# Router split moved from VectorE to ScalarE and GpSimd, and new work orders for the front of a cross-attention and expert kernel

## What is computed

```python
def _L0_xattn_ref(texto, imagen, Wq, bq, Wk, bk, Wv, bv):
    q = texto @ Wq + bq
    k = imagen @ Wk + bk
    v = imagen @ Wv + bv
    scores = jnp.einsum('bqd,bkd->bqk', q, k) * scale
    attn = jax.nn.softmax(scores, axis=-1)
    return jnp.einsum('bqk,bkd->bqd', attn, v)

def _L0_ffn_ref(x, w_router, w_gating, w_gate, w_up, w_down):
    router_probs = jax.nn.softmax(jnp.einsum('bsh,he->bse', x, w_router), axis=-1)
    gate_weights = jax.nn.softmax(jnp.einsum('bsh,he->bse', x, w_gating) / GATE_TEMP, axis=-1)
    g = jnp.einsum('bsh,ehf->ebsf', x, w_gate)
    u = jnp.einsum('bsh,ehf->ebsf', x, w_up)
    h = jax.nn.silu(g) * u
    expert_out = jnp.einsum('ebsf,efh->ebsh', h, w_down)
    cw = router_probs * gate_weights
    cw = cw / (jnp.sum(cw, axis=-1, keepdims=True) + 1e-09)
    return jnp.einsum('ebsh,bse->bsh', expert_out, cw)
x = x + _L0_xattn_ref(_layernorm(x, axis=-1), ctx_1024, ...)
x = x + _L0_ffn_ref(_layernorm(x, axis=-1), ...)
```

## Time and profile before

| | us |
|---|---|
| median of 3 runs | 983.49 (982.96 to 984.57) |
| profiled execution, its time | 983.63 |
| its span, first to last instruction | 981.8 |
| TensorE busy | 972.3 |
| VectorE busy | 751.7 |
| GpSimd busy | 671.1 |
| ScalarE busy | 483.8 |

### The profile page before, as it was taken

The page is one execution under the profiler, slowest core; times in us unless marked ns, Lnnn a source line. Parts: engine busy times, 40 slices in busy tenths (PEclk is TensorE's granted clock), DMA queues, the critical chain, the costliest instruction groups (busy, mean ns, idle before and its releaser), DMA issues.

```text
span 981.8 us, 16527 instructions
## 1 busy us (share of the span) xinstructions
PE 972.3 (99%) x6167; PEld 925.7 (94%) x6167; DVE 751.7 (77%) x1355; ACT 483.8 (49%) x857; POOL 671.1 (68%) x514
## 2 busy tenths in 40 slices
PE   8999999999999999999999999999999999999998
PEld 7899999999999999999999999999999999999998
DVE  6987456877788777787777877778877788777785
ACT  6788564453544444444535444444445454444441
POOL 3789976866767576676667675766767676767642
PEclk9999999999999999999999999999999999999999
DMA  8341140010101001010101010010100010100002
GB/s 213 85 140 46 36 150 22 22 43 3 43 22 43 23 22 43 22 44 23 36 9 44 22 44 22 22 43 22 44 22 24 21 44 23 43 22 23 1 1 76
DMA packets 37352, 40.63 MB, mean 41 GB/s; under 512 B 2644, under 2 KB 35272, under 8 KB 37272
## 3 DMA queue, kind: packets, MB, share of 16 engines
q1 hardware_dynamic: 37264, 39.58, 13.6%
q10 hardware_dynamic: 8, 0.00, 0.0%
HBM read 35.90 MB, written 3.67 MB: 40 GB/s over the span
## 4 chain that ended last, share of the span: by engine, by line
PE 97%; DMA 1%; DVE 1%; SPq 1%; issue 0%; ACT 0%; DVEq 0%
PE ps L280 94%; DMA w_raw<-in_L_ffn_w_up 1%; PE ps L1556 1%; PE ps L1584 1%; DVE wr_split L284 0%; DVE arena L284 0%; PE ps L1627 0%; PE ps L1601 0%; SPq L294 0%; PE ps L1545 0%; SPq L328 0%; PE ps L1652 0%; SPq L339 0%; SPq L324 0%; DVE xsacc L1264 0%
## 5 line engine op out<-in xcount | busy, mean ns | idle before, releaser
L280 PE MATMUL ps<-arena 128*128 128x256 f32 (+3 forms) x3120 | 415.2, 285 | 2.6 <-DVE arena L284 2.2
L280 PEld LDWEIGHTS ps<-arena 128*128 128x128 f32 (+2 forms) x3120 | 404.2, 190 | 9.7 <-DVE arena L1085 1.7
L488 POOL TENSOR_TENSOR arena<-shared,arena 128x448 fp32r<-128x448 f32 x196 | 250.8, 1295 | 192.6 <-ACT arena L825 185.7
L280 PE MATMUL ps<-xc_hi,w_hi 128*128 128x448 f32 x904 | 331.7, 367 | 0.0
L280 PE MATMUL ps<-xc_hi,w_lo 128*128 128x448 f32 x904 | 330.2, 365 | 0.0
L280 PE MATMUL ps<-xc_lo,w_hi 128*128 128x448 f32 x904 | 329.7, 365 | 0.0
L818 ACT ACTIVATE shared<-shared 128x448 f32<-128x448 f32 x180 | 101.4, 579 | 191.8 <-DVE shared L1204 124.9
L280 PEld LDWEIGHTS ps<-xc_hi,w_lo 128*128 128x128 f32 x904 | 169.8, 188 | 13.8
L280 PEld LDWEIGHTS ps<-xc_hi,w_hi 128*128 128x128 f32 x904 | 170.5, 189 | 10.5
L280 PEld LDWEIGHTS ps<-xc_lo,w_hi 128*128 128x128 f32 x904 | 170.6, 189 | 10.2
L1198 DVE TENSOR_TENSOR shared<-ps,shared 128x448 f32<-128x448 f32 x60 | 37.5, 624 | 110.9 <-PE ps L280 110.9
(11 more groups left out here) (152 smaller groups left out, 1103.4 us busy)
## 6 DMA issues: line engine op xcount, KB each, us to landing
early<-in_L_ffn_w_down SPq DMA_DIRECT2D x16, 512.0 KB, 4.0
shared<-in_ctx SPq DMA_DIRECT2D x16, 336.0 KB
w_raw<-in_L_ffn_w_gate SPq DMA_DIRECT2D x17, 256.0 KB, 2.9
w_raw<-in_L_ffn_w_up SPq DMA_DIRECT2D x17, 256.0 KB, 3.3
early<-in_L_ffn_w_gate SPq DMA_DIRECT2D x15, 256.0 KB, 2.8
early<-in_L_ffn_w_up SPq DMA_DIRECT2D x15, 256.0 KB, 3.2
x_dram<-xsacc SPq DMA_DIRECT2D x8, 224.0 KB, 2.7
xsacc<-x_dram SPq DMA_DIRECT2D x1, 1792.0 KB, 7.5
```

The lines of the kernel that those rows point to most:

```text
L280: ins = nc.tensor.matmul(dst, w, m, start=first and i == 0, stop=last and i == len(passes) - 1, skip_group_check=onto)
L488: nc.gpsimd.tensor_tensor(h[:, 1, j, at:at + TC], tile, h[:, 0, j, at:at + TC].bitcast(fp32), ALU.subtract).then_inc(hid_lo_done, 1)
```

## The change

Three things are done. The router's split leaves VectorE: its copy becomes ScalarE's `router_high`, its subtraction GpSimd's `router_low`. Its transfer, `load_router`, moves in the SP queue from behind the first context to behind the last part of x. And the hand-laid lists of calls of SP, GpSimd, ScalarE, VectorE and TensorE are written in another order, up to the first experts' tiles. The number of `keep_busy` calls stays ten; eight stood before `transpose_weights(1)`, now four do, and six stand between `queries(0)` and `transpose_ctx(3, 0)` (two before).

```diff
-            load_x(0)
             load_weights(0)
             load_weights(1)
+            load_x(0)
+            load_ctx_half(0, 0)
             load_x(1)
-            load_ctx_half(0, 0)
+            load_bv()
             load_ctx_half(0, 1)
+            load_ctx_half(1, 0)
+            load_set(0)
+            load_x(2)
+            load_ctx_half(1, 1)
+            load_wv()
+            load_x(3)
+            load_ctx(2, 0)
             load_router()
...
+            def router_low():
+                pool.wait_ge(wr_hi_done, 1)
+                nc.gpsimd.tensor_tensor(wr_split[:, :, 1, :], wr_raw[:], wr_split[:, :, 0, :].bitcast(fp32),
+                                        ALU.subtract).then_inc(wr_done, 1)
...
+            def router_high():
+                sc.wait_ge(router_in, 2 * DMA)
+                nc.scalar.copy(wr_split[:, :, 0, :], wr_raw[:]).then_inc(wr_hi_done, 1)
...
-            def split_router():
-                ve.wait_ge(router_in, 2 * DMA)
-                nc.vector.tensor_copy(wr_split[:, :, 0, :], wr_raw[:]).then_inc(wr_hi_done, 1)
-                ve.wait_ge(wr_hi_done, 1)
-                low(wr_split[:, :, 1, :], wr_raw[:], wr_split[:, :, 0, :]).then_inc(wr_done, 1)
```

More of the change, by code:

```diff
@@ L542, in _ @@
             root2(3)
+            cn_low(6, 1)
             norm2(3)
-            cn_low(6, 1)
+            low_part(0, "first")
             cn_low(7, 0)
-            low_part(0, "first")
+            add_bv(7)
             low_part(0, "second")
             cn_low(7, 1)
+            root2(4)
             low_part(0, "s13")
-            root2(4)
+            norm2(4)
+            sum_s4()
             low_part(0, "s2")
-            sum_s4()
-            norm2(4)
+            root2(5)
+            norm2(5)
             sum_of_set(3, 0)
@@ L864, in _ @@
             cn_high(2, 0)
+            router_high()
             ct_high(3, 0)
+            high_set(1)
             exponentials(2, 0)
-            cn_high(2, 1)
-            high_set(1)
-            pt_high(2, 0)
-            normalise(1)
-            ct_high(3, 1)
-            q_high(3)
-            exponentials(2, 1)
-            at_high(1)
+            exponentials(2, 1)
+            normalise(1)
+            q_high(3)
+            pt_high(2, 0)
+            ct_high(3, 1)
+            cn_high(2, 1)
+            cn_high(3, 0)
             pt_high(2, 1)
             norm1(4)
-            cn_high(3, 0)
             ct_high(4, 0)
@@ L1307, in _ @@
             m_low()
+            xt_low(0)
             both_biases()
@@ L1323, in _ @@
             neg_maximum(1, 0)
+            pt_low(0, 1)
             shift(1, 0)
-            pt_low(0, 1)
+            stats1(3)
+            ct_low(2, 0)
             invert_mass(0)
-            split_router()
-            ct_low(2, 0)
+            xt_low(2)
             neg_maximum(1, 1)
-            xt_low(2)
             shift(1, 1)
-            stats1(3)
             times_bk(2)
@@ L1337, in _ @@
             pt_low(1, 1)
+            invert_mass(1)
             at_low(0)
@@ L1779, in _ @@
             key_bias_row()
-            transpose_norm(0)
             transpose_ctx(0, 0)
@@ L1783, in _ @@
             query_bias()
+            transpose_norm(0)
             transpose_ctx(0, 1)
@@ L1786, in _ @@
             queries(0)
+            keep_busy(1)
+            keep_busy(1)
             transpose_ctx(1, 0)
+            transpose_norm(1)
+            keep_busy(1)
             scores(0, 0)
-            transpose_norm(1)
             scores(0, 1)
@@ L1822, in _ @@
             mix_ctx(2)
+            transpose_probs(3, 0)
+            queries(4)
             transpose_ctx(4, 1)
-            queries(4)
-            transpose_probs(3, 0)
+            transpose_probs(3, 1)
             values(1)
-            transpose_probs(3, 1)
+            scores(4, 0)
+            transpose_mix(2)
             transpose_ctx(5, 0)
-            transpose_mix(2)
-            scores(4, 0)
             transpose_norm(5)
-            transpose_norm2(0)
             scores(4, 1)
             mix_ctx(3)
+            transpose_ctx(5, 1)
             transpose_probs(4, 0)
-            transpose_ctx(5, 1)
+            transpose_norm2(0)
+            transpose_probs(4, 1)
             queries(5)
             values(2)
-            transpose_probs(4, 1)
             transpose_mix(3)
@@ L1842, in _ @@
             scores(5, 0)
+            transpose_norm(6)
             scores(5, 1)
-            transpose_norm(6)
             mix_ctx(4)
+            transpose_ctx(6, 1)
+            transpose_norm2(1)
             transpose_probs(5, 0)
-            transpose_norm2(1)
-            transpose_ctx(6, 1)
             queries(6)
```

349 lines of the change are left out of this document (167 added, 182 removed).

## The result

The changed kernel takes 978.12 us (median of 5, 977.99 to 979.23); the kernel before took 984.02 in the same session (median of 5, 982.96 to 984.83). The ratio is 0.9942, 95% interval 0.9928 to 0.9957.

The account below looks back on a forecast made before the run. TensorE, full from 40 to 970 us, bounds the kernel, so only the front can gain. -1.84 (wait) - 1.70 (clock) + 0.1 (short waits) + 0.5 (start to scores(1, 0)) = -2.9 us, from 983.63 to 980.7; range 978.9 to 983.0.

Parts of the forecast that it names:

- Part 1, the split: Split off VectorE ahead of ct_low(2, 0): TensorE's 1.84 us wait and 1.70 us of clock return, less 0.1.
- router_high and router_low: The split's replacements on ScalarE and GpSimd: zero cost for the copy, about 0.3 us for the subtraction.
- Part 2, the start: Up to queries(0): both weights load first, so it starts 0.35 us earlier, between 0.9 earlier and 0.3 later.
- the line of bytes: Pace of transfers, 5.2 us a MB, carried back to 1.34 MB: x's second part lands at 8 to 9.5.
- Part 3, to `scores(1, 0)`: From queries(0) to scores(1, 0): x's third part lands about 17.7, so +0.5 us, start included.
- both walks: New lists walked to scores(1, 0): 25.1 if x lands at 17.7, 24.25 if it holds nothing, against 24.59.
- Part 4: 36 to 140 us, same work reordered: zero cost, GpSimd's norm2(7) keeping 0.2 to 1 us of slack.
- E: Better: x lands in time and the start gives 0.9 us, 979.3 us; chance 0.10.
- A: Clock still falls: one half-rate stretch remains in the front, 1.7 us given back, 982.4 us; chance 0.14.
- B: GpSimd late: TensorE waits 1 to 1.5 us at transpose_norm2(4), (6) or (7), 982.1 us; chance 0.12.
- D: Slower: norm2(7) on GpSimd ends 4 us late and the clock falls (1.7), 986.4 us; chance 0.06.
- C: No net gain: x's third part lands at 19.5 or later, or its last holds stats1(3), 983.3 us; chance 0.10.

Follow-up runs that it names:

- e1: The kernel before with only the router's split moved, to ScalarE and GpSimd, all orders as before: 980.31 us.
- e3: The kernel before with the router's split moved to ScalarE and GpSimd and its transfer behind the last x, orders as before: 979.87 us.
- e6: The kernel before with the split still on VectorE, but placed behind q_low(0), where GpSimd is idle: 980.03 us.
- e11_delay_b: e1 with 22 unread statistics instructions (4.33 us) on VectorE where the split had stood: 983.74 us.
- a0_changed: The changed kernel itself, timed and profiled again in another session: 978.58 us.
- e10: e1 with 12 unread statistics instructions (2.40 us) on VectorE where the split had stood: 980.95 us.
- e4: The changed kernel with the router's split back on VectorE, behind invert_mass(0): 978.47 us.
- e14: e3 with the changed kernel's lists up to mix_ctx(1) (36 us), the lists of before behind: 979.38 us.
- e7_no_fill: The changed kernel without the six keep_busy calls behind queries(0): 978.98 us.
- e5: The changed kernel with the router's transfer put back behind the first context: 978.80 us.
- e12: e3 with the new order up to queries(0), without four keep_busy, and xt_high(1) ahead of high_set(0): 979.00 us.
- e16: e3 with the changed kernel's lists up to just ahead of scores(1, 0): 980.14 us.
- e2_load_moved: The kernel before with only the router's transfer moved behind the last part of x: 982.49 us.

## Why the prediction was wrong

**What bounds the kernel**: right. The gain is in the first 40 us, by the idle time and the clock, and nothing was lost behind.

**Part 1, the split**: right in its sum, wrong in its make-up. Forecast -3.5 and 0.1 back; measured -3.1 (e1), -3.5 (e3), -3.4 (e6). The wait of 1.84 us is gone, as written. But the 1.70 us "returned by the clock" was a row of TensorE's read as a cost of the kernel. It is a term that was mis-sized: beside this stall the fall is worth some 0.4 to 0.7 us, as `e11_delay_b` and the 64 long executions of before show. From `scores(1, 0)` to the mark the stall costs 3.6 us (14.7 against 11.1 in e1); in `e11_delay_b`, without the fall, 3.3: 1.77 and 0.73 us of waits (the second at `transpose_ctx(3, 0)`, which the slow clock had only covered) and 0.8 that no row names. Two errors of about one size and opposite sign made the sum good: I had counted the clock too high, and had let the delay of 4.38 us end with its first wait. The step `ct_low(2, 0)` "comes 2.2 us earlier" with equal starts was right: it started 7.16 us behind `scores(1, 0)` and starts 4.91 behind it now. It came 4.0 earlier in all, because the start was earlier by 1.8.

I had also taken the kernel before for one kernel with one time. It had two, most likely according to whether the subtraction waited for one `cn_low` or two.

**router_high and router_low**: right, 0.22 and 0.25 us, no cost.

**Part 2, the start**: this step failed, on a value chosen. Forecast -0.35 for `queries(0)`, with a bound at -0.9; measured -1.05, and -0.94 in `a0_changed` (12.72). Over the four profiles with each kind of front (before, e1, e10, e11: 13.39 to 14.23; the changed kernel twice, e4, e14: 12.53 to 12.72) it is -1.2. Its first half held: VectorE's `weights_low(1)` is no longer behind `stats1(1)`, and `merged_weights` starts 1.63 us earlier. Timeline of VectorE in the kernel before, then in the kernel after, `weights_low(1)` (128x512) and `stats1(1)`:

```profile
7.87 0.75 DVE L1032 BATCH_NORM_STATS2 bn<-xsacc 112x6 f32<-112x256 f32 x2 [0.18 <-DMA xsacc<-in_x]
...
9.21 0.68 DVE L284 TENSOR_TENSOR xc_hi<-ps,xc_hi 128x512 fp32r<-128x512 f32 x1
...
7.64 0.68 DVE L284 TENSOR_TENSOR xc_hi<-ps,xc_hi 128x512 fp32r<-128x512 f32 x1
8.24 0.74 DVE L1043 BATCH_NORM_STATS2 bn<-xsacc 112x6 f32<-112x256 f32 x2
```

The second half did not: x's second part, put at 8 to 9.5 by the line of bytes, was there by 8.24, and VectorE did not wait for it. From 8.24 the steps took 4.3 us to the end of `xt_low(0)` at 12.55, close to the 4.0 counted. So the durations were right and the landing too late by up to a microsecond.

**Part 3, to `scores(1, 0)`**: this step failed as well. Forecast +0.5 for the start of `scores(1, 0)`, part 2 included, so +0.85 for the stretch itself; measured -1.77, and -0.56 in `a0_changed` (24.03). Over the same four profiles of each kind `scores(1, 0)` is 1.1 us earlier (24.3 to 23.2), so the stretch itself is about as long as before (+0.1): of the 1.6 us by which the term was off, half is part 2's and half this stretch's. The 1.77 of the first pair has luck in it. The two profiles separate the errors. In `a0_changed` x part 3 did hold VectorE, as forecast, and yet `scores(1, 0)` came at 24.03 and not at 25.1: 0.6 of that microsecond is the start's, the rest the walk's. In the first profile x landed at 15.3 and held nothing, and the other 1.2 us were there. `e7_no_fill` is like it, e4 and e5 lie between. The landing at 17.7, from a line through two landings of the earlier trace rows, was never reached; 17.1 was the latest seen. I had written down both walks and chosen the pessimistic one because of the bytes. A landing that varies by 1.8 us in one program could not carry that choice.

**The sum.** With the two terms as measured over several profiles, -3.7 for the stall (14.7 us from `scores(1, 0)` to the mark before, 11.0 now) and -1.1 for the start of `scores(1, 0)`, the same sum gives -4.8 us and 978.8, near the 978.58 of the changed kernel in its second session. So +0.5 in place of -1.1 is the term that put the time below the range; the 0.5 us between the two sessions is beside that.

**Part 4**: right in that nothing is lost. `norm2(7)` ended at 112.9 and TensorE used it at 114.39, 1.5 us of slack as before. The times were not: 116.5 and 117 were forecast, and the first doesn't follow from its own terms (121.8 less 3.3 less 3 is 115.5). Timeline of GpSimd, then of TensorE, in the kernel after, for the earlier trace rows:

```profile
110.49 2.43 POOL L415 TENSOR_SCALAR early<-xsacc,mv,rstd 112x256 f32<-112x256 f32 x2
...
114.39 0.55 PE L1631 MATMUL ps<-ident,early 112*128 112x112 f32 x4
```

**The rivals**: the result is nearest to E (x in time, part 2 at its good end), which had 0.10 and gave 979.3, because it took `scores(1, 0)` 0.9 us earlier where the profile has 1.77, and the stall at 3.4 us where it is 3.7. A did not happen in a profile: the clock is 1.00 in the front of every one with the new orders. In four single executions of e12, e14 and e16 the mean clock was 0.998; where in them it fell isn't known. (The full clock that A reads from the earlier trace rows isn't in them; a window from 0 to 5 us has it.) B and D did not: GpSimd is never waited for. C's mechanism, x late, occurred in three of the five profiles above, by 0.73 us at most, and the mark was at most 1.25 us later, not the whole gain. So the mechanisms were on the page and the weights were wrong: four of the five rivals lay on the side of less gain, and the low end of the range cut through E's own tail.

## What to carry to other kernels

Price a stall by what the next engine does with the time given back, not by the rows of the engine that stalls: here a slow TensorE clock for the most part filled a wait for VectorE, and removing one cause in two ways did not pay twice. A mark, the start of one operation ahead of which all versions have the same work, tells where a gain was made: span less mark was constant to 0.2 us in all profiles but one and put the whole gain in the front. But the start itself varies by over a microsecond, so a stretch between two marks is the sharper measure (11.0 to 11.1 us in eleven profiles). Before a short VectorE instruction with two SBUF inputs is moved to another engine, look whether GpSimd is busy beside it; moving it to another place on its own engine was as good (e6, and e4 in the new orders).

## What the runs showed of the hardware

- A subtraction of 32 columns from SBUF to SBUF on VectorE took 0.19 us with GpSimd idle, 1.78 when it waited for one GpSimd instruction of 1.8 us, and 3.56 for two in a row. The one wait was seen in a profile of `e2_load_moved`, the two in that of the kernel before; the times of both kernels fall in two groups 2.8 to 2.9 us apart. The copy of the same 32 columns took 0.17 us with GpSimd idle, 0.79 and 0.57 where it ended with GpSimd's `low_set(0)`.
- `ct_low`, which reads one input from PSUM, took 0.94 us beside GpSimd's `low_set(0)` and `cn_low` in `e6_split_early`, and 0.93 in the earlier trace rows, where it starts as `cn_low` ends: it wasn't held up.
- A wait of TensorE of 1.84 us was followed by a fall of the granted clock to 0.50 in one kernel, one of 1.77 us by none in the profile of another.
- One program's transfer of 448 KB of x landed 8.4 and 10.0 us after its issue, with the same transfers ahead. The router's 16 KB, in whichever place of the queue, had no cost that could be measured.
